# Gated cross attention with a top-2 mixture of experts: table entries and expert ordering spread over more steps, tiles 0 and 1 gathered and turned in the last batch, expert weights loaded by ScalarE

## The reference

```python
def xattn(x, latents, ...):                 # x: context 32x375x256, latents: 32x112x256
    x, lat = layer_norm(x, ...), layer_norm(latents, ...)
    q = lat @ Wq; kv = concat([x, lat], 1) @ Wkv; k, v = split(kv)   # 16 heads of 64
    attn = softmax(q k^T * 64 ** -0.5)
    return (attn v) @ Wout
def ffn(x, gate_w, w1, b1, w2, b2):         # 3584 tokens, 8 experts, top 2
    scores = softmax(x @ gate_w); top, idx = top_k(scores, 2); top /= sum(top)
    y[e] = gelu(x @ w1[e] + b1[e]) @ w2[e] + b2[e]       # 256 -> 1024 -> 256
    return sum_k top[k] * y[idx[k]]
x = x + tanh(g_xattn) * xattn(ctx, layernorm(x), ...)
x = x + tanh(g_ffn) * ffn(layernorm(x), ...)
```

## Time and profile before

| what | value |
|---|---|
| time, median of 3 runs | 1769.18 us (1767.91 to 1771.01) |
| the profiled execution's own time | 1766.65 us |
| its span, first to last instruction | 1764.9 us |
| mean granted TensorE clock | 0.977 |
| TensorE busy | 1650.7 us (94%) |
| GpSimd busy | 1283.2 us (73%) |
| VectorE busy | 1256.8 us (71%) |
| ScalarE busy | 1229.0 us (70%) |
| DMA, hardware queue of SyncE | 57.8% of 16 engines' span |

### The profile page before, as it was taken

How to read it: one execution, slowest core, us unless ns; L and a number is a source line. 1 busy time by engine, 2 the same in 40 slices (tenths; PEclk the granted TensorE clock), 3 DMA queues, 4 the chain that set the end, 5 groups by cost and what they waited for, 6 DMA issues and landing times.

```text
span 1764.9 us, 42362 instructions
## 1 busy us (share of the span) xinstructions
PE 1650.7 (94%) x14914; PEld 1151.9 (65%) x14914; DVE 1256.8 (71%) x3004; ACT 1229.0 (70%) x2803; POOL 1283.2 (73%) x1448
## 2 busy tenths in 40 slices
PE   3999999999999999999999999998885988999997
PEld 1556666666666666666666666665554877888886
DVE  6777777777877777777777787788755775655553
ACT  3687888878778887877788878876665555544442
POOL 4477878787878888888888888898575464555443
PEclk9999999999999999999999999999987998999999
DMA  4268776777677768777776767755569756544443
GB/s 147 62 128 145 148 147 136 149 147 146 138 136 151 140 140 151 145 141 138 138 143 138 147 128 145 141 106 100 104 109 224 201 117 150 96 76 70 70 68 31
DMA packets 634297, 226.80 MB, mean 129 GB/s; under 512 B 573930, under 2 KB 624914, under 8 KB 633708
## 3 DMA queue, kind: packets, MB, share of 16 engines
q1 hardware_dynamic: 617964, 207.41, 57.8%
q0 software_dynamic: 15552, 16.67, 6.1%
q10 hardware_dynamic: 576, 0.01, 0.0%
HBM read 67.72 MB, written 16.83 MB: 48 GB/s over the span
## 4 chain that ended last, share of the span: by engine, by line
PE 81%; DVE 9%; ACT 4%; issue 2%; SPq 2%; DMA 1%; POOL 1%; ACTq 0%; POOLq 0%; DVEq 0%
PE proj_ps L1426 38%; PE scores_ps L1602 10%; PE scores_ps L1469 10%; PE proj_ps L1615 9%; PE pv_ps L1504 5%; PE tail_ps L1526 4%; PE pv_ps L1506 2%; DVE v_sb L1230 2%; ACT v_sb L875 2%; DVE passed L1081 2%; PE scores_ps L1426 1%; PE proj_ps L1576 1%; ACT p_space L795 1%; DVE k_lo L1224 1%; ACT g_space L910 1%
## 5 line engine op out<-in xcount | busy, mean ns | idle before, releaser
L629 POOL TENSOR_TENSOR p_parts<-p_space,p_parts 112x487 f16<-112x487 f32 x512 | 561.6, 1120 | 114.2 <-ACT p_parts L804 113.4
L795 ACT ACTIVATE p_space<-scores_ps,shift 112x487 f32<-112x487 f32 x508 | 335.6, 665 | 15.7 <-DVE passed L1081 9.2
L1081 DVE TENSOR_SCALAR_CACHE_REDUCE passed<-scores_ps 112x487 f16<-112x487 f32 x502 | 302.5, 660 | 25.0 <-PE scores_ps L1469 24.9
L861 ACT ACTIVATE k_hi<-proj_ps 128x488 fp32r<-128x488 f32 x250 | 144.6, 578 | 224.1 <-PE proj_ps L1426 223.9
L804 ACT ACTIVATE p_parts<-p_space 112x487 f16<-112x487 f32 x512 | 276.6, 608 | 0.0
L1230 DVE SCALAR_TENSOR_TENSOR v_sb<-proj_ps,v_sb 128x512 f16<-128x512 f32 x251 | 173.4, 691 | 144.1 <-ACT v_sb L875 144.1
L910 ACT ACTIVATE g_space<-scores_ps,b_sb,undo 128x256 f32<-128x256 f32 x280 | 139.4, 561 | 177.3 <-PE scores_ps L1602 176.0
L1504 PE MATMUL pv_ps<-v_sb,pt_space 128*128 128x128 f16 x2048 | 217.8, 221 | 15.7 <-DMA pt_space<-p_parts 15.3
L1224 DVE TENSOR_TENSOR k_lo<-proj_ps,k_hi 128x488 fp32r<-128x488 f32 x250 | 165.9, 664 | 82.9 <-ACT k_hi L861 81.0
L1602 PE MATMUL scores_ps<-xt_space,arena 128*128 128x256 f16 x1680 | 194.5, 277 | 19.4 <-issue 11.6
L1426 PE MATMUL proj_ps<-kv_hi,wkv_hi 128*128 128x488 f16 x500 | 187.2, 374 | 12.8 <-DVE v_sb L1230 9.9
(11 more groups left out here) (285 smaller groups left out, 3541.1 us busy)
## 6 DMA issues: line engine op xcount, KB each, us to landing
w_part<-in_L_ffn_w_dram SPq DMA_DIRECT2D x64, 256.0 KB, 3.6
arena<-in_L_ffn_w_dram SPq DMA_DIRECT2D x28, 512.0 KB, 5.2
ctx_sb<-in_ctx_dram SPq DMA_DIRECT2D x32, 375.0 KB
pt_space<-p_parts SPq DMA_TRANSPOSE x256, 4.0
x_sb<-in_x_dram SPq DMA_DIRECT2D x32, 112.0 KB
res_sb<-in_x_dram SPq DMA_DIRECT2D x32, 112.0 KB, 5.4
out_dram<-x_sb SPq DMA_DIRECT2D x32, 112.0 KB
xn_dram<-xn SPq DMA_DIRECT2D x32, 112.0 KB
```

What stands on the lines that cost most here:

```text
L629: pool.tensor_tensor(p_parts[0:LQ, p % PS, h, 1, 0:LK], p_f[0:LQ, p % 2, h, 0:LK], p_parts[0:LQ, p % PS, h, 0, 0:LK], ALU.subtract).then_i ...
L795: act.activation(p_f[0:LQ, p % 2, h, 0:LK], score_bank(p, h)[0:LQ, 0:LK], ACT.Exp, bias=shift[0:LQ, p // 2 % 2, n:n + 1], scale=-1.0, accu ...
L1081: dve.tensor_scalar(passed_of(p, h), score_bank(p, h)[0:LQ, 0:LK], P_SHIFT, None, ALU.add, ALU.min, accum_out=shift[0:LQ, p // 2 % 2, n:n ...
```

## The change

`entry_turns` writes one column of entries in each odd step from 152 on, instead of one or two in some steps; none is written from step 240 to 255, and from 256 on two a step. The last group of batches (28 to 31) becomes two groups of two, so that four of its eight columns are written at steps 265 and 266 and the other four at 281 and 282. `order_experts`, `tiles_of_experts` and `tile_rows` are spread over 7 steps (234 to 240) instead of 2. The turning and copying of the lists for tiles 0 to 13 moves to step 244. The gathers of tiles 0 and 1 go from step 253 to steps 247 and 249, their transposes from behind step 255 (tile 0) and from iteration -1 (tile 1) to steps 251 and 253. The loads of the expert weights are issued by ScalarE instead of SyncE, one or two at a time by their own table, and unit 0 goes through another buffer (`g_space`) at step 240. The splits are spread anew.

```diff
-GROUPS = ((0, 8), (8, 16), (16, 22), (22, 25), (25, 28), (28, 32))
+GROUPS = ((0, 8), (8, 16), (16, 22), (22, 25), (25, 28), (28, 30), (30, 32))
...
-        room = (1 if t < 208 else 2) if t % NP in (3, 7) else 2 if t >= 224 and t % NP in (1, 5) else 0
-        if t >= PAIRS - NP:
-            room = 4 if t < PAIRS else 8
+        room = 1 if t % NP in (3, 7) or t % 2 == 1 and t >= 152 else 0
+        if t >= PAIRS:
+            room = 2
+        elif t >= NP * 28 + 16:
+            room = 0
...
-SPLITS = {-3: (0,), -2: (1,), -1: (2, 3), 1: (4,), 2: (5,), 3: (6,), 4: (7,), 6: (8,), 7: (9,), 8: (10,), 9: (11,), 11: (12,), 12: (13,), 13: (14,), 15: (15,),
-          16: (16,), 17: (17,), 19: (18,), 24: (19,), 25: (20,)}
+SPLITS = {-7: (0,), -2: (1,), -1: (2,), 0: (3,), 1: (4,), 2: (5,), 3: (6,), 4: (7,), 7: (8,), 9: (9,), 10: (10,), 11: (11,), 13: (12,), 14: (13,), 15: (14,), 17: (15,),
+          18: (16,), 19: (17,), 21: (18,), 24: (19,), 25: (20,)}
...
-TILE_SPLITS = {6: (21, 22, 23), 7: (24, 25), 8: (26, 27), 9: (28, 29), 10: (30, 31)}
-LOADS = {t + 1: [u + 4 for u in units if u + 4 not in (8, 9, 10, 11)] for t, units in SPLITS.items() if t < LAST_STEP}
-LOADS[PAIRS - 4] = [0, 1, 2, 3]
-LOADS[PAIRS + 5] = [8, 9, 10, 11]
-TILE_LOADS = {6: (24, 25, 26, 27), 7: (28, 29), 9: (30, 31)}
+TILE_SPLITS = {6: (21,), 7: (22, 23), 8: (24, 25), 9: (26, 27), 10: (28, 29), 11: (30, 31)}
+LOADS = {-16: (0,), -4: (1, 2), -3: (3,), -2: (4,), 0: (5,), 1: (6,), 2: (7,), 4: (8,), 5: (9, 10), 6: (11,), 9: (12,), 11: (13,), 12: (14,), 13: (15,),
+         14: (16,), 15: (17,), 16: (18,), 18: (19,), 19: (20,), 20: (21,), 22: (22,), 26: (23,)}
+LOADS = {PAIRS + n: units for n, units in LOADS.items()}
+TILE_LOADS = {6: (24, 28, 29), 7: (25,), 8: (26, 27), 11: (30, 31)}
...
-SLOTS_STEP = PAIRS - 4
+READ_STEP = CHAIN + 17
+SLOTS_STEP = CHAIN + 20
+GATHER_STEPS = (PAIRS - 9, PAIRS - 7)
+FILL_STEPS = (PAIRS - 5, PAIRS - 3)
...
+            def load_unit(u):
+
+                if u == 0:
+                    act.wait_ge(order_known, 1)
+                    act.wait_ge(kvlo_done, 2 * NB)
+                if u == 1:
+                    act.wait_ge(pv_done, PAIRS - NP)
+                if u == 8:
+                    act.wait_ge(pv_done, PAIRS)
+                if u in (24, 28):
+                    act.wait_ge(out_done, NB)
+                if 5 <= u < 28 and u // 4 != 2:
+                    act.wait_ge(unit_low, u - 3)
+                if u >= 30:
+                    act.wait_ge(unit_low, u - 1)
...
+            def order_experts(turn):
...
+                if 0 <= t - ORDER_STEP < 3:
+                    order_experts(t - ORDER_STEP)
+                if t == ORDER_STEP + 3:
                     tiles_of_experts(0.0)
+                if t == ORDER_STEP + 4:
                     by_slot(slot_tiles, tiles_f)
+                if t == ORDER_STEP + 5:
+                    tile_begins()
+                if t == ORDER_STEP + 6:
                     tile_rows(0)
```

More of the change, by code:

```diff
@@ L556, in step @@
                     sp.dma_start(xn_rows[ob * LQ:(ob + 1) * LQ], xn_parts(ob).bitcast(F32)).then_inc(stored[ob % 2], 16)
-                for u in LOADS.get(t, ()):
-                    load_unit(u)
+                for n in range(2):
+                    if t == FILL_STEPS[n]:
+                        turn(n)
                 if t == PAIRS + 2:
@@ L739, in step @@
                     read_table(0)
[L740 to L745 removed]
+                for n in range(2):
+                    if t == GATHER_STEPS[n]:
+                        for s in range(2):
+                            pool.wait_ge(stored[s], (FIRST_BATCHES + 1 - s) // 2 * 32)
+                        pool.wait_ge(slots_known, 1)
+                        gather(n)
             for t in STEPS:
@@ L944, in _ @@
                     step(t)
+                for u in TILE_LOADS.get(i, ()):
+                    load_unit(u)
                 for u in TILE_SPLITS.get(i, ()):
```

103 lines of the change are left out of this document (41 added, 62 removed).

## The result

| | kernel before | changed kernel |
|---|---|---|
| median | 1769.78 us (4 runs) | 1781.92 us (1777.51 to 1781.96, 4 runs) |
| ratio | 1 | 1.0063 [1.0047, 1.0079] |
| profiled execution, its span | 1766.65, 1764.9 us | 1777.51, 1775.7 us |

The change makes the kernel 0.63% slower, some 11 us. The prediction said 1759 us (1746 to 1772): wrong by 23 us, and outside its range.

What follows compares the result with a forecast made beforehand. The prediction took TensorE to be the bound, with stalls in the last batch and tiles. Its terms, -5 - 14 - 5.7 + 2.5 - 5 + 17.4 = -9.8 us, took 1766.65 to 1756.9, as a median 1759 us (range 1746 to 1772).

Steps and rivals of the forecast that it cites:

- term B: Last batch: fewer entries on GpSimd and loads off SyncE's queue start hidden(0) 14 us earlier (bounds 8 and 18).
- rival 2: Last batch: transposes stay slow while loads are in flight, whoever issues them; gain there only 4 us, time 1769; chance 0.16.
- A: Step 235: spreading the expert ordering over 7 steps ends VectorE's hold-up of TensorE; 5 us off (bounds 0 and 6).
- B's ring: Last batch, after pair 249: each two pairs take 6.8 us; three turns end pair 255 at 1331.2, 16.0 us earlier.
- C: Tiles 1 to 4: ScalarE's wait for a unit goes, 5.7 us off; four new entries before tile 4's gathers cost 2.5.
- D: Tile 8: four of its eight entries are gone, 5 us off; the rest of the stall, 5 us, stays.
- E: Tiles 9, 11 and 13: the last weight units come too late behind `result`; a loss of 17.4 us (bounds 11 and 22).
- Rival 3: Tiles 2 to 6: ScalarE blocked before loads that wait for `unit_low`; three unhidden waits cost 17 us, time 1776; chance 0.18.

Runs made afterwards that it cites:

- e6: Changed kernel with the loads of units 1 to 3 issued at step 255, 4 at 256, and splits of 1 to 3 at 256; ratio 1.0067 to the kernel before.
- e5: Changed kernel with each load of units 1 to 7 issued twice, the second into a spare DRAM tensor; 1788.58 us, ratio 1.0110 to the kernel before.
- e7: Changed kernel with all loads issued by SyncE, at the changed kernel's steps, ahead of the tiles' transposes; 1763.95 us, ratio 0.9977 to the kernel before.
- e9: Kernel before with the loads of units 0 to 23 issued by ScalarE at SyncE's steps; ratio 1.0029 to the kernel before.
- e13: Changed kernel with the loads of units 0 to 7 issued by SyncE, the rest by ScalarE; ratio 1.0076 to the kernel before.
- e14: Changed kernel with the loads of units 8 to 31 issued by SyncE, 0 to 7 by ScalarE; ratio 1.0010 to the kernel before.
- e10: Kernel before with the expert ordering spread over 7 steps and the tiles' lists turned at step 244; ratio 0.9971 to the kernel before.
- e8: Changed kernel with the expert ordering in two steps (234 and 235) again; 1790.28 us, ratio 1.0122 to the kernel before.
- e11: Changed kernel with loads by SyncE and the last units split and loaded in the kernel before's iterations; 1748.94 us, ratio 0.9889 to the kernel before.

## Why the prediction was wrong

**The step that failed is in term B**: that the loads' leaving SyncE's queue frees the transposes ("Gone are ... in SyncE's order, the four loads and the 7.04 us transpose behind them"), and that each load by ScalarE costs ScalarE 0.53 us and nobody anything. What the runs showed in its place: a load in ScalarE's queue takes part at once, beside whatever transposes and gathers SyncE and GpSimd have under way, while a load in SyncE's queue stands behind the transposes issued ahead of it. e6 shows the slowing (3.06 us for two pairs' becomes 8.23 and 10.00), e5 suggests that it grows with the bytes, e7 shows that the order in one queue avoids most of it (3.4 us over the usual instead of 8.9), and in e9 it costs the kernel before some 5 us, with an interval that reaches no change. The price of ScalarE's issuing is 15 us of the 23 us that the forecast was off; the wait of ScalarE before unit 22 is a part of it, at most 3.5 us. The rule of the Trainium skill ("DMA: Bandwidth & Descriptors", Issuing engines are not separate DMA queues), given against the change, held in its main point: the transfers share the engines whoever issues them. That another issuer saves only issue time was too kind here: the same loads by ScalarE cost 15 us.

That was rival 2, with 0.16. It got B right in size (4 us, measured 3.3: from the scores of pair 248 to hidden(0) 50.8 us before, 47.5 after), but it priced the last batch alone. The same collisions in tiles 2 to 8 were in none of the cases, and e13 and e14 say that the larger part is there.

**Point by point.**

- *A*, 5 us: borne out by the medians, 5.1 in e10. Inside the changed kernel e8 says 10 us, but with intervals that overlap. Of the 5.26 us stall at 1226.44 that stood ahead of the one I priced, the spreading alone leaves 4.44 us (e10), the respaced entries alone 3.52 (e8), and both together 0.69.
- *B's ring*: mis-sized, and its end near the forecast by luck. Pair 255's low halves end at 1332.8, forecast 1331.2, but that forecast did not have the earlier start in it: the scores of pair 248 came 6.5 us earlier than before. From the end of pair 249 the three turns took 26.1 us, where 3 x 6.8 = 20.4 were forecast and 32.5 were taken before. They take 25.9 us in e7 as well, so the loads' issuer is not why. hidden(0) did not wait for this: it stands behind the product of pairs 252 and 253, and that waits for SyncE. With SyncE's loads hidden(0) starts at 1334.6. That is 15.5 us of the 19 forecast for A and B; B itself, counted from the scores of pair 248, is some 9 of 14.
- *C*: ScalarE's 8.79 us wait shrank to 2.30 us, but hidden(2) to hidden(4) took 34.3 us instead of 30.3. Two waits came in: `base` for batch 30's transpose, 2.40 us, a wait that the split group makes and that I had not counted, and 4.97 us before hidden(3), whose gathers were issued at 1361.1 and whose transposes SyncE could issue only at 1377.3, 16.2 us later (9.5 in e7).
- *D*, 5 us: nothing by itself (hidden(7) to hidden(8) 21.1 us, 20.8 before); with SyncE's loads 15.8, so the 5 us are there.
- *E*, 17.4 us: mechanism and place right for all three (3.02, 3.43, 4.42 us for 3.5, 3.5 and 5.2), slow matmuls at two of three; 14.2 us by the stretches, 15.6 by e11 against e7.
- *Rival 3*, ScalarE blocked: it came once, not three times. ScalarE stands before the load of unit 22, and TensorE waits 1.86 us more before hidden(7) and computes it 1.7 us slower. The rival's time of 1776 was near for another reason.

Had term B's step held, the time would have been near the forecast: the changed kernel with SyncE's loads is at 0.9977, 1766 us by the ratio, for 1759. In part that is luck again. In the traces it is 5.9 us better than before at hidden(14), where 9.8 were forecast: B is some 5 us short, C and D together gain 2.6 us instead of 8.2, and E costs 12.2 instead of 17.4.

**What stays open**: why e13 loses in tiles 2 to 8 more than the changed kernel does, and whether it is the gathers or the tiles' transposes that the loads hold up most; no run separates the two, and the traces show both. At tile 8 it is the transposes: from gathers to transposes 5.9 us (5.4 in e7), from transposes to hidden(8) 9.2 (4.1). At tile 3 it is the gathers (16.2 and 9.5 us). The parts `entry_turns` and the early gathers were not run alone.

## What to carry to other kernels

Before moving transfers to another engine's queue, list what short, awaited transfers are under way at that time in the old queue: the old queue's order was also a priority, and a free issuer gives it up. A slow transfer behind a load says nothing about the queue; it can be the load itself. Look, too, at what each issue waits for: on its new engine it holds up all that stands behind it. And look where the last unit of a table becomes ready, instruction by instruction: one that stands, on its engine, behind an instruction that waits for the limiting engine's newest result is late by construction, in every iteration whose next tile wants it at once.
